# Two reorderings in a fused decoder layer: a down product cut in two around a set of transposes, and attention's output sum taken in two halves

## The reference: what is computed

```python
x = x + retention(layernorm(x), Wq, Wk, Wv, W1, W2, gn_w, gn_b)     # 8 heads of 32, decay mask, gate
x = x + cross_attention(layernorm(x), ctx, xWq, xbq, ..., xWo, xbo)  # 16 heads of 16, causal softmax
x = x + expert_ffn(layernorm(x), w1, b1, w2, b2)                     # 8 experts, 256 tokens each, gelu, 1024 wide
```

## Time and profile before

| | us |
|---|---|
| median of three runs | 350.64 (350.55 to 352.16) |
| the profiled execution, its own time | 350.86 |
| its span, first to last instruction | 349.1 |
| TensorE busy in the span | 326.7 (94%) |
| VectorE busy | 253.2 (73%) |
| ScalarE busy | 238.8 (68%) |
| GpSimd busy | 160.6 (46%) |

### The profile page before, as it was taken

The page is one execution under the profiler, slowest core; times in us unless marked ns, Lnnn a source line. Parts: engine busy times, 40 slices in busy tenths (PEclk is TensorE's granted clock), DMA queues, the critical chain, the costliest instruction groups (busy, mean ns, idle before and its releaser), DMA issues.

```text
span 349.1 us, 9369 instructions
## 1 busy us (share of the span) xinstructions
PE 326.7 (94%) x3471; PEld 275.0 (79%) x3475; DVE 253.2 (73%) x552; ACT 238.8 (68%) x585; POOL 160.6 (46%) x144
## 2 busy tenths in 40 slices
PE   8788788999999999999999999999999998979696
PEld 3556556898789888888889888888789887858696
DVE  5664766687767886787768886788768877574784
ACT  4362556679858877679858877678858877797360
POOL 3645441190845457190846357181836363651100
PEclk9999999999999999999999999999999999999999
DMA  6990100413005500523005400513014300404000
GB/s 144 277 283 5 33 0 4 150 31 123 4 16 182 152 2 4 161 68 115 0 19 176 150 0 6 179 57 103 0 35 163 120 2 17 152 1 138 0 32 30
DMA packets 22458, 27.36 MB, mean 78 GB/s; under 512 B 2944, under 2 KB 20160, under 8 KB 22432
## 3 DMA queue, kind: packets, MB, share of 16 engines
q1 hardware_dynamic: 21616, 26.91, 24.5%
q10 hardware_dynamic: 816, 0.10, 0.2%
HBM read 24.51 MB, written 2.10 MB: 76 GB/s over the span
## 4 chain that ended last, share of the span: by engine, by line
PE 73%; issue 9%; DVE 9%; POOL 4%; ACT 3%; DMA 1%; ACTq 0%; DVEq 0%; POOLq 0%
PE c L1217 20%; PE a L1217 15%; PE b L1217 14%; PE b1k L1217 7%; PE b1k L1381 6%; PE b2k L1217 3%; DVE negmax L917 2%; PE c L1408 2%; PE a L1232 1%; POOL w_lo L465 1%; DVE probT L924 1%; DVE scD L898 1%; DMA wk_c<-in_L_attn_Wk 1%; PE b L1232 1%; PE b2k L1232 1%
## 5 line engine op out<-in xcount | busy, mean ns | idle before, releaser
L452 POOL TENSOR_TENSOR rstA<-varA,minus_half 128x16 f32<-128x16 f32 x8 | 23.4, 2928 | 62.5 <-DVE varA L1056 62.5
L601 ACT ACTIVATE prob<-b,negmax 128x128 f32<-128x128 f32 x124 | 35.8, 387 | 15.2 <-DVE negmax L917 15.2
L1381 PE MATMUL b1k<-ident,prob 128*128 128x128 f32 x256 | 39.5, 277 | 5.4 <-DVE probT L924 2.2
L465 POOL TENSOR_TENSOR w_lo<-w_in,w_hi 128x512 fp32r<-128x512 f32 x28 | 35.4, 1298 | 10.0 <-ACT w_hi L563 6.1
L563 ACT ACTIVATE w_hi<-w_in 128x512 fp32r<-128x512 f32 x64 | 37.8, 639 | 2.6 <-PE b L1217 2.6
L459 POOL TENSOR_TENSOR w_lo<-w_in,w_hi 128x512 fp32r<-128x512 f32 x28 | 35.0, 1284 | 8.3 <-ACT w_hi L563 6.6
L1381 PEld LDWEIGHTS b1k<-ident,prob 128*128 128x128 f32 x256 | 28.8, 141 | 11.4 <-ACT prob L601 6.3
L1217 PE MATMUL c<-xTC_hi,w_hi 128*128 128x256 f32 x108 | 31.9, 295 | 0.5
L452 POOL TENSOR_TENSOR rsC<-mvC,minus_half 128x2 f32<-128x2 f32 x8 | 5.7, 715 | 57.5 <-DVE mvC L854 57.5
L917 DVE TENSOR_REDUCE negmax<-b 128x4 f32<-128x512 f32 x31 | 21.3, 687 | 14.7 <-PE a L1217 8.2
L1217 PE MATMUL c<-xTC_lo,w_hi 128*128 128x256 f32 x108 | 30.5, 282 | 0.0
(11 more groups left out here) (296 smaller groups left out, 1118.7 us busy)
## 6 DMA issues: line engine op xcount, KB each, us to landing
w_in<-in_L_ffn_w SPq DMA_DIRECT2D x16, 1024.0 KB, 5.7
x_in<-in_x SPq DMA_DIRECT2D x8, 256.0 KB, 2.8
c_in<-in_ctx SPq DMA_DIRECT2D x8, 256.0 KB, 2.9
out<-x2b SPq DMA_DIRECT2D x7, 256.0 KB, 2.2
b_cur<-in_L_ffn_b SPq DMA_DIRECT2D x8, 128.0 KB, 3.0
W_sb<-in_L_attn_W SPq DMA_DIRECT2D x2, 256.0 KB, 5.0
decay_sb<-in_decay SPq DMA_DIRECT2D x1, 512.0 KB, 3.8
mask_bf<-mask_bf SPq DMA_DIRECT2D x3, 128.0 KB, 7.5
```

What stands on the lines that cost most here:

```text
L452: pool.tensor_tensor(out, in_, minus_half[:, 0:n], ALU.pow).then_inc(s_out, 1)
L465: pool.tensor_tensor(w2_lo[:, part, :], w2_in[:, part, :], w2_hi[:, part, :].bitcast(F32), ALU.subtract).then_inc(s_w2lo, 1)
L601: ins = nc.scalar.activation(prob[:, u % PR, g, :], score_banks[u][:, g * P:(g + 1) * P], ACT.Exp, bias=negmax[:, u, g:g + 1], scale=-1.0)
L1381: ins = nc.tensor.transpose(b1k[:, g * P:(g + 1) * P], prob[:, u % PR, g, :], ident[:, :])
```

## The change

First, piece 4 of the down product is cut into its two values of `f`. The first three matmuls stay in place, ahead of `prob_transposes(2)`; the other three move behind `prob_transposes(3)`, ahead of `down(5)`. This is in steps 2 to 7.

Second, attention's output of groups 0 to 5 and of group 7 goes to two banks, one for each 128 tokens, each with its own increment. VectorE adds and takes `bn_stats` of the first half when that half is there, then adds the second half; the statistics at the start of the next step are left with the second half's `bn_stats`. Group 6 stays as it was.

```diff
-            def statistics(step, src, stat, mv, s_ln):
+            def statistics(step, src, stat, mv, s_ln, left=range(NB)):
-                for b in range(NB):
+                for b in left:
                     nc.vector.bn_stats(stat[:, b, :], src[:, b, :]).then_inc(s_ln, 1)
...
-                def ffn_statistics():
+                def ffn_statistics(left=(1,)):
                     dve.wait_ge(s_x2, c + 1)
-                    statistics(c, x2, statC, mvC, s_lnC)
+                    statistics(c, x2, statC, mvC, s_lnC, left)
...
+                def add_attention_halves(step, nth, banks):
+                    dve.wait_ge(s_yB_half, nth)
+                    dve.wait_ge(s_x1b, step + 1)
+                    if later(step):
+                        dve.wait_ge(s_x2b, step)
+                    nc.vector.tensor_tensor(x2[:, 0, :], banks[0][:, 0:D], x1b[:, 0, :], ALU.add)\
+                        .then_inc(s_x2_half, 1)
+                    dve.wait_ge(s_x2_half, nth)
+                    nc.vector.bn_stats(statC[:, 0, :], x2[:, 0, :]).then_inc(s_lnC, 1)
+                    dve.wait_ge(s_yB, step + 1)
+                    nc.vector.tensor_tensor(x2[:, 1, :], banks[1][:, 0:D], x1b[:, 1, :], ALU.add).then_inc(s_x2, 1)
...
-                    ffn_statistics()
+                    ffn_statistics(range(NB))
...
-                    add_attention(b, b1k)
+                    add_attention_halves(b, STEPS - 1, (b1k, c0))
...
-                    add_attention(b, b0)
+                    add_attention_halves(b, b + 1, (b0, b2k))
...
+                def attention_out_halves(step, banks):
+                    pe.wait_ge(s_attTlo, step + 1)
+                    for bk, bank in enumerate(banks):
+                        tok = slice(bk * P, (bk + 1) * P)
+                        for k in range(C):
+                            ins = mm_split(bank[:, 0:D], [t[:, k, tok] for t in (attT_hi, attT_lo)],
+                                           [w[:, k, :] for w in (xWo_hi, xWo_lo)], start=(k == 0), stop=(k == C - 1))
+                        ins.then_inc(s_yB if bk else s_yB_half, 1)
...
-                def down(piece):
+                def down(piece, halves=(0, 1)):
...
-                    for f in (2 * quarter, 2 * quarter + 1):
-
+                    for half in halves:
+                        f = 2 * quarter + half
...
-                    attention_out(b, b1k)
+                    attention_out_halves(b, (b1k, c0))
...
                     down(3)
-                    down(4)
+                    down(4, (0,))
...
                 if do_c:
+                    down(4, (1,))
                     down(5)
...
-                    attention_out(b, b0)
+                    attention_out_halves(b, (b0, b2k))
```

More of the change, by code:

```diff
@@ L295, in decoder_kernel @@
         s_x2 = signal("s_x2")
+        s_yB_half = signal("s_yB_half")
+        s_x2_half = signal("s_x2_half")
         s_w1 = signal("s_w1")
```

## The result

| | before | after |
|---|---|---|
| median of 11 runs, same chips | 351.85 us | 349.83 us |
| profiled execution, its own time | 350.86 us | 348.83 us |
| its span | 349.1 us | 347.0 us |

The ratio of the times is 0.9944 (95% interval 0.993 to 0.9957). The forecast was 348.6 against 350.64, a ratio of 0.9942, and 348.8 for the profiled execution. Over half of the runs of either kernel (8 of 11 before, 6 of 11 after) lie 1.1 to 1.3 us above the others, because TensorE's clock falls for a few microseconds at the end (last experiments); both profiles shown here are without that fall. So both medians of the table are of runs with the fall, while the 350.64 that the forecast started from was a run without it. Compared with their like, the runs after are shorter by 1.80 us without the fall (350.64 to 348.84, medians) and 1.9 with it (351.89 to 350.00).

What follows compares the result with a forecast made beforehand. TensorE, busy 94%, was taken to bound the kernel, with a 0.39 us stall per step and 2.47 us idle at the end. 1.6 + 0.45 = 2.05 us off gives 348.6 us (profiled 348.8), range 347.9 to 349.9.

Steps and rivals of the forecast that it cites:

- The hole before T4: PE idle 0.39 us before probability transposes' fourth set (from 0), which waits for VectorE's copy of transposed probabilities.
- part one: In steps 2 to 7, moving three down matmuls brings the scores 0.27 us earlier per step, 1.6 us in all.
- the third limit: Fourth mask on PE, ahead of the scores, needs ScalarE's exponentials; it can move 0.22 to 0.31 us earlier.
- my lower bound of 0.22: Smallest shift of the fourth mask in step 5, in us: 0.36 less a release of 0.14.
- my 0.14: Upper bound, in us, from the exponentials' end to the fourth mask, read from VectorE's copy before PE's transposes.
- T2's limit: Set 2 (from 0) of probability transposes needs VectorE's copy of set 1; at most 0.29 us earlier in step 5.
- Part two in the steady steps: Six half sums of attention's output on VectorE: 0 us, between 0 and a loss of 0.1 per step.
- Part two at the end: Last half sum, step 8: statistics ready 0.45 us earlier, between 0.43 and 0.51, the upper with VectorE's sums overlapping.
- The sum: Whole kernel: 1.6 us from part one plus 0.45 at the end, 2.05 us in all.
- the slower one: Rival: in the steady steps the split sum delays `x2` and PE waits for it; some 352.5 us, chance 0.03.
- The end gives nothing: Rival: at the end VectorE's split `h_lo` work and GpSimd's addition may set the pace; 349.0 us, chance 0.07.
- The scores hardly move: Rival: releases in PE's row of mask waits cut the scores' shift to 0 to 0.15 us; 349.7 us, chance 0.25.

Runs made afterwards that it cites:

- last experiments: Eight matmuls over zeros put into PE's last idle time, in the changed kernel (ratio to before 0.9923) and in it with the loop written out (0.9896).
- short square: Stage A's square on ScalarE over 32 instead of 512 columns, in the changed kernel and the one before: loop steps 38.88 and 39.06 us.
- halves alone: Only the half sums of attention's output added to the kernel before, down piece 4 whole and in its old place: ratio to before 0.9974.
- cut alone: Only the cut and moved down piece 4 added to the kernel before, attention's output summed whole: ratio to before 0.9969.

## Why the prediction was right, and where it was not

- **The hole before T4** was there, and is gone (0.39 to 0.03 us); nine matmuls stand in front of T4. Leaving the three out changes nothing, moving six lengthens the step from 38.88 to 39.15: the reading of the hole as room for 0.35 us of work, set by VectorE's chain, is shown.
- **The size of part one** was the term that was off: 6 x 0.27 = 1.6 us forecast, 234.13 - 232.72 = 1.41 measured (0.31, 0.20, 0.20, 0.21, 0.16 and 0.33). The failing step is the third limit, "the fourth mask", and with it "what is late next is the fourth mask, which ScalarE's exponentials hold back". It is late, but not for ScalarE's exponentials. In the loop steps T2 gave its 0.30 us as worked out (203.59 - 0.79 against 202.50, the 0.79 being what T1 had already moved). Then the first mask follows T2 by 0.56 instead of 0.53, and the fourth follows the first by 0.11 instead of 0.04: 0.30 - 0.03 - 0.07 = 0.20. The short square excludes the exponentials, and writing the loop out restores the 0.1 us. What in the loop holds the mask stays open. That the value landed near my lower bound of 0.22 was luck, and so was that the mask starts 0.15 us behind the exponentials, as my 0.14 would have it: with the short square it is 0.58.
- **T2's limit** by VectorE's copy of T1 was right, with its 0.14 us. In the loop that copy itself starts 0.09 later after T1 than in the written-out steps.
- **Part two in the steady steps**: forecast 0, measured 0 (234.13 and 234.12 with the halves alone). The order of the reasons holds as well: `x2` comes earlier, the normalisation does not.
- **Part two at the end**: forecast 0.45 between 0.43 and 0.51, measured 0.52. From the start of the first half sum to the end of the second `bn_stats` it takes 326.49 - 324.81 = 1.68 us, as at the upper bound (328.00 - 326.32): VectorE's instructions overlap, the second sum starts 0.35 after the `bn_stats` in front of it. I should have taken the bound with the overlap, which the timeline of before showed.
- **The sum**: the last transposes come 330.88 - 328.85 = 2.03 us earlier, of which 1.41 are part one, 0.52 part two, 0.07 were there at step 1 already and 0.03 arise between step 7 and the end; forecast 2.05. One term was too large by 0.2, one too small by 0.07, and 0.1 come from no part of the change. So the near hit of the profile (348.83 against 348.8) is partly luck. Without the clock's fall the runs show 1.80 us less instead of 2.05.
- **The time itself**: the median of 349.83 lies only just inside the range from 347.9 to 349.9. The sum knew nothing of the clock's fall, which adds some 1.1 us; it started from a run without it. That the ratio, 0.9944, comes so near the forecast 0.9942 also owes something to the different shares of runs with the fall; 348.84 against 350.64 is 0.9949.
- **The rivals**: the slower one, that the split sum holds `x2` back, is refuted by the halves alone. "The end gives nothing" is refuted by the same run. "The scores hardly move" had the right place, a cost inside PE's row of mask waits, but a tenth of a microsecond and not three, and only in the loop.
- **The Trainium skill** ("Perfetto Trace Analysis", Optimizing Scalar/DVE Operations) says both that larger operations are better on a saturated engine and that breaking one up can let the work end sooner where it causes bubbles. The trace agrees with the second: seven more VectorE instructions (559 instead of 552, 254.3 instead of 253.2 us busy), no cost in the steps, and 0.52 us where a bubble was. The first is not tested here, as VectorE is busy for 73%.

## What to carry to other kernels

A hole in front of an instruction can be filled with work that now stands ahead of the chain that makes the hole: moving it lets the chain start earlier and fills the hole at once, but only by as much as the hole holds, so cut the piece to size. Split an operation where its consumer sits in an idle time, and do not expect anything of it where the consumer has another input that comes later. When identical steps gain differently, look at what differs in how they are issued, here loop against written out, before blaming the data they wait for.

## What the runs showed of the hardware that I had not expected

- In the loop a step costs 0.10 us more than the same step written out (39.07 against 38.97 before the change), and 0.24 in the changed kernel (38.88 against 38.64), where PE waits for VectorE's copy ahead of T2. VectorE's copy starts 0.73 us after the transposes begin in the loop and 0.63 to 0.64 outside it. Which part of the loop costs this is not shown.
- Behind PE's single idle time of 1.95 to 2.47 us near the end the granted clock fell in many executions of the same kernel (in 5 of 12 with the halves alone, in 10 of 12 with the cut alone), to 0.50 for some 3 us, which costs 1.1 to 1.3 us. Eight matmuls over zeros in that time removed the fall in all twelve runs of the two kernels that have them. PE's earlier idle time of 1.41 us, ahead of 309.20 us in the changed kernel, left the clock at 1.00.
